# 128 rows a transfer in three unrolled loops of gathers and scatters (a graph and mixture-of-experts kernel)

## The reference, cut to what matters

```
# layer 0, graph step: two table rows for each node, by its degrees
x + z_in[in_deg] + z_out[out_deg] + cent_term + vor_term + sum3d

# layer 1, experts: 8 experts, the best 2 of each node, 256 -> 512 -> 256
xn = layernorm(x) * gamma + beta
top-2 of xn @ Wr gives two experts and two shares for each node
y_e = gelu(xn @ W1[e] + b1[e]) @ W2[e] + b2[e]
x + share0 * y_(expert 0) + share1 * y_(expert 1)
```

## Time and profile before

| what | value |
|---|---|
| median of 3 runs | 7661.86 us (7650.2, 7661.86, 7663.13) |
| the profiled execution | 7653.44 us |
| its span, first to last instruction | 7651.7 us |
| mean granted clock of TensorE | 0.787 |
| POOL busy | 3770.9 us, 49% |
| PE busy | 3976.6 us, 52% |
| DVE busy | 3494.0 us, 46% |
| DMA packets | 406511, 665.78 MB, mean 87 GB/s |

### The profile page before, as it was taken

The page is one execution under the profiler, slowest core; times in us unless marked ns, Lnnn a source line. Parts: engine busy times, 40 slices in busy tenths (PEclk is TensorE's granted clock), DMA queues, the critical chain, the costliest instruction groups (busy, mean ns, idle before and its releaser), DMA issues. The chain is left out here.

```text
span 7651.7 us, 94951 instructions
## 1 busy us (share of the span) xinstructions
PE 3976.6 (52%) x18034; PEld 3067.9 (40%) x18035; DVE 3494.0 (46%) x6616; ACT 690.7 (9%) x1705; POOL 3770.9 (49%) x4068
## 2 busy tenths in 40 slices
PE   0005664566300488728936666666666566415980
PEld 0004553344100488617824444444444344214770
DVE  8889999522310266651134444444444242631112
ACT  0000001122100000002210000000000012212220
POOL 0027777777777673000037777777777500043016
PEclk9999999997555699859956676677677589657995
DMA  1013333333333577400023333333333500112113
GB/s 45 0 46 101 101 105 100 96 103 100 100 100 104 173 251 235 146 0 0 0 72 104 104 105 103 103 104 104 104 103 104 85 5 0 52 41 63 63 56 100
DMA packets 406511, 665.78 MB, mean 87 GB/s; under 512 B 230847, under 2 KB 260719, under 8 KB 393799
## 3 DMA queue, kind: packets, MB, share of 16 engines
q0 software_dynamic: 172768, 374.98, 17.3%
q1 hardware_dynamic: 233703, 290.37, 13.7%
HBM read 518.80 MB, written 145.91 MB: 87 GB/s over the span
## 5 line engine op out<-in xcount | busy, mean ns | idle before, releaser
L1394 POOL DMA_INDIRECT rows<-xn_rows,pw_in x1664 | 1610.5, 968 | 523.4 <-issue 490.5
L532 POOL DMA_INDIRECT rows_by_src<-ring,stage x1563 | 1515.7, 970 | 483.8 <-issue 462.9
L1527 PE MATMUL pg<-rows,hot 128*125 128x256 f32 x3328 | 1272.8, 535 | 786.7 <-DMA rows<-xn_rows,pw_in 389.4
L1527 PEld LDWEIGHTS pg<-rows,hot 128*125 128x125 f32 x3328 | 824.6, 266 | 1224.3 <-issue 1085.4
L993 PE MATMUL pw<-hot,win 128*128 128x125 f32 x3968 | 502.0, 294 | 685.0 <-DVE hot L948 577.7
L993 PEld LDWEIGHTS pw<-hot,win 128*128 128x128 f32 x3968 | 497.1, 210 | 690.4 <-issue 690.4
L1412 DVE TENSOR_TENSOR agg<-agg,pg 125x256 f32 x832 | 349.1, 420 | 715.8 <-PE pg L1527 702.1
L1453 DVE TENSOR_TENSOR hot<-ids,pw_in 128x250 f32<-128x250 int32 x832 | 345.5, 416 | 549.0 <-issue 507.9
L948 DVE SCALAR_TENSOR_TENSOR hot<-win,win_base,iota_f 128x1000 f32<-128x1000 f32 x248 | 322.2, 1300 | 567.1 <-issue 567.1
L705 PE MATMUL phist<-hi,lo 128*125 128x50 bf16 x3136 | 413.9, 281 | 219.4 <-DVE hi L555 219.4
L705 PEld LDWEIGHTS phist<-hi,lo 128*125 128x125 bf16 x3136 | 370.5, 222 | 264.1 <-issue 257.1
(11 more groups left out here) (404 smaller groups left out, 6179.9 us busy)
## 6 DMA issues: line engine op xcount, KB each, us to landing
win<-rows_by_src SPq DMA_DIRECT2D x248, 516.0 KB, 4.8
ring<-in_edge_attr SPq DMA_DIRECT2D x97, 1024.0 KB
rows<-xn_rows,pw_in POOLq DMA_INDIRECT x1664, 2.8
rows_by_src<-ring,stage POOLq DMA_INDIRECT x1563
XT<-moe_rows SPq DMA_DIRECT2D x56, 256.0 KB, 2.6
moe_results<-XT POOLq DMA_DIRECT2D x56, 256.0 KB, 2.4
pw_in<-pairs_by_dst SPq DMA_DIRECT2D x832, 2.0 KB
e_w<-in_L_ffn_W SPq DMA_DIRECT2D x16, 512.0 KB
```

Source lines behind the costliest of these rows:

```text
L532: pool.indirect_dma_start(rows_d, bass.IndirectOffsetOnAxis(ap=stage[:, h * HC + j:h * HC + j + 1].bitcast(U32), axis=0), ring4[:, h, j, : ...
L1394: pool.indirect_dma_start(rows[:, (2 * (s % RU) + r) * D:(2 * (s % RU) + r + 1) * D], None, xn2_d, bass.IndirectOffsetOnAxis(ap=pw_in[:, s ...
L1527: mm = pe.matmul(pg[0:P, s % 4, 0:D], hot[:, ((s % 4) * 2 + r) * P:((s % 4) * 2 + r + 1) * P], rows[:, (2 * (s % RU) + r) * D:(2 * (s % RU ...
```

## The change

In all three places the index tile has 128 partitions instead of 125, and so has the tile that rows are gathered into. Three spare rows ride along in each transfer: in the gathers they read row 0 of the table (the index tiles are cleared first), in the scatter each writes to a row of its own behind the used part of `moe_rows`, which grows by 12800 rows. The index is taken from `z_idx`, `pos_x` and `pos_y` where DVE wrote it, and the scatter reads its rows from `XT` where ACT keeps them; the staging copies, the `xr` copies by ACT and their semaphores are gone. The loops are Python loops with constant wait values. The z rows have four buffers instead of two, with three tiles gathered ahead.

Added: POOL clears `XT[96:128]` (32 partitions by 12800 numbers) at the head of the experts' block one, ahead of the clearing of `zero`, and ACT waits for it before it stores into `XT`; POOL fills `pos_x` with an `iota` and clears `pos_y`; a clearing of `z_idx` in the first section.

```
-    moe_x_d = nc.dram_tensor("moe_rows", (2 * N + MW, D), ...)
+    moe_x_d = nc.dram_tensor("moe_rows", (2 * N + MW + 128 * NT * 2, D), ...)
# first section
+            sp.wait_ge(pads_set, 8)
+            pool.memset(z_idx[:], 0).then_inc(pads_set, 1)
# z gathers
-            def gather_z(t, u):
-                ch.step(pool.tensor_copy(z_stage[:, 2 * u:2 * u + 2], z_idx[:, bass.ds(t * 2, 2)]))
+            def gather_z(t):
+                if t >= ZU:
+                    pool.wait_ge(z_added, t - ZU + 1)
+                u = t % ZU
                 for k, name in enumerate(("L0_gnn_z_in", "L0_gnn_z_out")):
                     pool.indirect_dma_start(z_rows[...], None, a[name],
-                        bass.IndirectOffsetOnAxis(ap=z_stage[:, 2 * u + k:2 * u + k + 1].bitcast(U32), axis=0)
+                        bass.IndirectOffsetOnAxis(ap=z_idx[:, 2 * t + k:2 * t + k + 1].bitcast(U32), axis=0)
                         ).then_inc(z_rows_in[u], 16)
+            def add_z(t):
+                u = t % ZU
+                pool.wait_ge(z_rows_in[u], 32 * (t // ZU + 1))
+                pool.tensor_tensor(Rt(t), Rt(t), z_rows[0:P, 2 * u * D:(2 * u + 1) * D], ALU.add).then_inc(z_in_added, 1)
+                pool.wait_ge(z_in_added, t + 1)
+                pool.tensor_tensor(Rt(t), Rt(t), z_rows[0:P, (2 * u + 1) * D:(2 * u + 2) * D], ALU.add).then_inc(z_added, 1)
+            for t in range(ZU - 1):
+                gather_z(t)
+            for t in range(NT):
+                if t + ZU - 1 < NT:
+                    gather_z(t + ZU - 1)
+                add_z(t)
# experts, block one, POOL
+                pool.memset(XT[96:128, :], 0.0).then_inc(spare_set, 1)
+                pool.wait_ge(spare_set, 1)
                 pool.memset(zero[:], 0.0).then_inc(zero_set, 1)
+                pool.iota(pos_x[:], pattern=[[128, NT * 2]], base=2 * N + MW, channel_multiplier=1).then_inc(spare_set, 1)
+                pool.memset(pos_y[:], 0).then_inc(spare_set, 1)
                 pool.wait_ge(placed, 1)
-                def scatter(t, u, i):
-                    at(pool, xr_ready, t + 1, passed["pool"])
-                    ch.step(pool.tensor_copy(stage[:, 2 * u:2 * u + 2], pos_x[:, bass.ds(t * 2, 2)]))
+                pool.wait_ge(xn_kept, NT)
+                for t in range(NT):
                     for k in range(2):
-                        pool.indirect_dma_start(moe_x_d, ...stage[:, 2 * u + k:2 * u + k + 1]..., xr[:, u * D:(u + 1) * D], None)
+                        pool.indirect_dma_start(moe_x_d, ...pos_x[:, 2 * t + k:2 * t + k + 1]..., XT[:, t * TS:t * TS + D], None)
# experts, block one, ACT
+                act.wait_ge(spare_set, 1)
-                def send(t, u, i):
-                    if later(t):
-                        at(act, row_sent[u], i * 32, passed["act"])
-                    act.copy(xr[:, u * D:(u + 1) * D], kept(t)).then_inc(xr_ready, 1)
-                tiles(act, send)
# experts, block three, POOL
-                    ch.step(pool.tensor_copy(stage[:, 2 * u:2 * u + 2], pos_y[:, bass.ds(t * 2, 2)]))
+                for t in range(NT):
+                    u = t % 4
+                    if t >= 4:
+                        pool.wait_ge(yg_used, t - 3)
                     for k in range(2):
                         pool.indirect_dma_start(yg[...], None, moe_y_d,
-                            ...stage[:, 2 * u + k:2 * u + k + 1]...)
+                            ...pos_y[:, 2 * t + k:2 * t + k + 1]...)
```

More of the change, by code:

```diff
@@ L875, in program @@
         win_in = [sem(f"win_in{s}") for s in range(U)]
-        z_rows_in = [sem("z_rows_in0"), sem("z_rows_in1")]
-        z_added = sem("z_added")
+        z_rows_in = [sem(f"z_rows_in{u}") for u in range(ZU)]
+        z_in_added, z_added = sem("z_in_added"), sem("z_added")
         accs_ready = sem("accs_ready")
@@ L1912, in _ @@
             def _(pool):
-                ch = chain("pool", pool)
+                pool.memset(XT[96:128, :], 0.0).then_inc(spare_set, 1)
+                pool.wait_ge(spare_set, 1)
                 pool.memset(zero[:], 0.0).then_inc(zero_set, 1)
+                pool.iota(pos_x[:], pattern=[[128, NT * 2]], base=2 * N + MW, channel_multiplier=1).then_inc(spare_set, 1)
+                pool.memset(pos_y[:], 0).then_inc(spare_set, 1)
                 pool.wait_ge(placed, 1)
-                def scatter(t, u, i):
-                    at(pool, xr_ready, t + 1, passed["pool"])
-                    ch.step(pool.tensor_copy(stage[:, 2 * u:2 * u + 2], pos_x[:, bass.ds(t * 2, 2)]))
+                pool.wait_ge(xn_kept, NT)
+                for t in range(NT):
                     for k in range(2):
-                        pool.indirect_dma_start(moe_x_d, bass.IndirectOffsetOnAxis(ap=stage[:, 2 * u + k:2 * u + k + 1].bitcast(U32), axis=0),
-                                                xr[:, u * D:(u + 1) * D], None).then_inc(row_sent[u], 16)
-                tiles(pool, scatter, ch, 2)
-                for u in range(2):
-                    pool.wait_ge(row_sent[u], 32 * (NT // 2))
+                        pool.indirect_dma_start(moe_x_d, bass.IndirectOffsetOnAxis(ap=pos_x[:, 2 * t + k:2 * t + k + 1].bitcast(U32), axis=0),
+                                                XT[:, t * TS:t * TS + D], None).then_inc(row_sent, 16)
+                pool.wait_ge(row_sent, 16 * 2 * NT)
             @block.vector
@@ L2000, in pick @@
                     ch.step(dve.tensor_reduce(got[:], p3, AX.X, ALU.add))
-                    ch.step(dve.tensor_copy(out[:].rearrange("p (t k) -> p t k", k=2)[:, :, k], got[:]))
+                    ch.step(dve.tensor_copy(out[0:P, :].rearrange("p (t k) -> p t k", k=2)[:, :, k], got[:]))
+                dve.wait_ge(spare_set, 3)
                 for k in range(2):
@@ L2185, in program @@
         with ExitStack() as c3:
-            yg = sbuf(c3, "e_yg", [P, 4 * 2 * D])
-            stage = sbuf(c3, "e_stage2", [P, 4 * 2], I32)
+            yg = sbuf(c3, "e_yg", [128, 4 * 2 * D])
             yg_in = [sem(f"e_yg_in{u}") for u in range(4)]
@@ L2210, in _ @@
             def _(pool):
-                ch = chain("pool", pool)
-                def gather(t, u, i):
-                    if not isinstance(t, int) or t >= 4:
-                        at(pool, yg_used, t - 3, passed["pool"])
-                    ch.step(pool.tensor_copy(stage[:, 2 * u:2 * u + 2], pos_y[:, bass.ds(t * 2, 2)]))
+                for t in range(NT):
+                    u = t % 4
+                    if t >= 4:
+                        pool.wait_ge(yg_used, t - 3)
                     for k in range(2):
                         pool.indirect_dma_start(yg[:, (2 * u + k) * D:(2 * u + k + 1) * D], None, moe_y_d,
-                                                bass.IndirectOffsetOnAxis(ap=stage[:, 2 * u + k:2 * u + k + 1].bitcast(U32), axis=0)
+                                                bass.IndirectOffsetOnAxis(ap=pos_y[:, 2 * t + k:2 * t + k + 1].bitcast(U32), axis=0)
                                                 ).then_inc(yg_in[u], 16)
-                fours(pool, gather, ch, 1)
             @block.vector
```

44 lines of the change are left out of this document (12 added, 32 removed).

## The result

The changed kernel takes 7561.42 us (median of 4 runs, 7553.38 to 7568.24) against 7662.49 for the kernel before in the same company: ratio 0.987, 95% interval 0.9853 to 0.9887. That is 101 us less, where 131 were forecast. The range ended at 7562 us; the ratio, carried over to the 7661.86 us of the runs shown, gives 7562.3, just above it. The profiled execution took 7562.53 us with a span of 7560.8, 90.9 us less than the span before.

The account below looks back on a forecast made before the run. POOL's issue of indirect DMAs was taken to bound scatters and last block; 66 + 64 + 2 - 1 = 131 us less gave 7522 against the profiled 7653.4, 7531 carried to the median; forecast 7529, range 7505 to 7562.

Parts of the forecast that it names:

- The reading of the bound: Scatters and last block: POOL's issue of indirect DMAs sets the pace, 3.8 us a tile in each.
- harmless wait: Last block: POOL's wait for the tile four back is met near 6.5 us, before the buffer is needed at 10 us.
- The new price: Scatters and last block: a 128-row transfer costs POOL 1.25 us with idle, bounds 1.24 and 1.49.
- Scatters: Experts' scatters, first staging copy to last issue: 190.6 us becomes 125.6; 66 us less with landing, bounds 42 and 67.
- Last block: Last block's gathers: 188.8 us becomes 124.1, landing about 1 less, 2 off for queueing; 64 us less, bounds 35 and 67.
- z: Hidden z gathers: dropping 25.3 us of POOL's copies makes the stage 2 us less, bounds 3 more to 4 less.
- Its cover: z gathers: POOL would be done near 2850 us, still ahead of DVE's tables, which run to 3190.
- the port: z gathers: POOL's work slows DVE's tables by 12.4 us over the stage; fewer copies give back 2 us.
- Added work: Head of the experts' block one, mainly clearing `XT[96:128]` beside DVE's statistics: costs 1 us, bounds 0 and 5.
- A: Last block: the DMA engines take POOL's place; at 3.0 us a tile 25 us are lost, 7554; chance 0.12.
- B: Scatters and last block: issues get no cheaper with 128 rows; 200 transfers at 0.24 us, 48 us, 7577; chance 0.05.
- C: Scatters: unpaced transfers hold each other up in POOL's issue; slower from 2.6 us each, 7684 at 2.8; chance 0.01.
- D: Unrolled code must be fetched and POOL stands at times: 5 to 10 us, 7537; within the forecast case's 0.80.

Follow-up runs that it names:

- r3: Kernel before with the scatters' part alone (128 rows, unrolled, cleared `XT[96:128]`, larger `moe_rows`): 7593.29 us, ratio 0.9919.
- r9: Kernel before with the z gathers' part alone (128 rows, unrolled, four buffers, memset of `z_idx`), timed again: 7668.14 us, ratio 1.0035.
- r14: Kernel before with the z gathers unrolled, four buffers, indices from `z_idx`, but 125 rows and no memset: 7678.65 us, ratio 1.0039.
- r12: The whole change, timed again beside the parts, against the kernel before: 7549.58 us, ratio 0.9868.
- r10: Kernel before with the scatters' and last block's parts, without the z part: 7525.54 us, ratio 0.9838.
- r15: Changed kernel plus 15 one-column POOL memsets after that of `z_idx` and 11 after the z gathers: 7548.65 us, ratio 0.9868 to the kernel before.
- r16: Kernel before with the scatters' and last block's parts, without the z part, once more: 7534.81 us, ratio 0.985.
- r5: Kernel before with the z gathers' part alone, including the memset of `z_idx`, on a slower chip: 9832.81 us, ratio 1.0013.
- r13: Kernel before with only `z_idx` at 128 partitions and cleared by one more POOL memset: 7650.29 us, ratio 0.9999.
- r7: Changed kernel with 125 rows in each of the three transfers, on a slower chip: 9704.69 us, ratio 0.9892 to the kernel before.
- r11: Kernel before with 480 one-column POOL memsets behind the z loop: 7650.48 us, ratio 1.0.
- r17: Kernel before with 243 one-column POOL memsets behind the z loop, on a slower chip: 9813.73 us, ratio 1.0002.
- r18: Kernel before with the z part's three more semaphores and larger `z_rows` allocated but unused, on a slower chip: 9801.54 us, ratio 0.9993.
- r2: The changed kernel, unchanged, timed again against the kernel before: 7548.08 us, ratio 0.9863.

## Why the prediction was wrong

**The reading of the bound** was right: POOL's row of instructions set both stages, and shortening it shortened them. `yg_used` stayed the harmless wait it was taken for: POOL waited 1.5 us for DVE in the whole last block.

**The new price.** Forecast 1.25 us a transfer; measured 127.5 / 99 = 1.288 in the scatters and 1.284 in the last block. The idle of 0.30 was right. The issue was read at its tight end (0.95 in a stretch of the gathers) and came at 0.98, as the means of the earlier trace rows had said. 0.036 x 200 is 7 us of the shortfall.

**Scatters**: 66 forecast, 57.6 in the trace (62.3 - 4.7) and 57.7 in r3. Beside the pace, the term had landing 0.9 us shorter, which came as 1.7, and no drain: that is a step that failed too, a wait put at nothing. POOL's drain of 100 transfers of 128 rows took 6.2 us more. It wasn't seen because the prediction followed the chain to the landing and stopped there; the barrier's own instructions were not read.

**Last block**: 64 forecast, 60.8 in the trace between its issues. POOL's drain ends the program there:

```profile
L2175 POOLq DRAIN  x1: 14070/14070/14070, 7546.5 to 7546.5; - x1
L2175 SPq DRAIN  x1: 7/7/7, 7559.7 to 7559.7; - x1
```

It starts while POOL still has issues to make and ends 8.22 us after the last of them does, in all nine traces with this block, the same 8.22 us as in block one, with the landing and SP's last store beside it. SP is done at 7559.7, 8.3 us behind the last issue instead of 8.8, but the program ends 9.4 us behind it instead of 9.0. So the 1 us that earlier landing was to give did not arrive. (The term's own lower bound is added up wrongly: 188.8 - 147.8 + 1 - 5 is 37, not 35; nothing rests on it.)

**z: "2 us less (3 more to 4 less)" is the step that failed.** Its cover was read rightly: POOL's last z addition ends at 2852 us instead of 2965, near the 2850 that were forecast; the hot rows take 606.1 and 609.4 us, and over the 14 profiled executions of 7535 to 7675 us 596 to 615 with the unrolled z transfers and 598 to 608 without. Groups by line of POOL in the changed kernel, 2583 to 2966 us, beside the earlier trace rows:

```profile
L910 POOL DMA_INDIRECT z_rows<-in_L_gnn_z_in,z_idx x50 | 65.9, 1318 | 13.5 <-POOL R L919 12.5 <-issue 1.1
L910 POOL DMA_INDIRECT z_rows<-in_L_gnn_z_out,z_idx x50 | 59.5, 1189 | 15.2 <-issue 15.2
```

DVE's tables in two stretches, with and without POOL's z transfers, beside the earlier trace rows:

```profile
2583.00:2850.00 267.00, 142.47 (x104) 0.85 0.79 263
2860.00:3190.00 330.00, 170.17 (x136) 0.91 0.67 218
```

The copies are gone, and the z transfers are done in 267 us instead of 382. A table takes 142.47 / 104 = 1.370 us beside them and 170.17 / 136 = 1.251 after: 0.119 x 104 = 12.4 us in all, just what it was. So the port, by which POOL's work slows DVE's, gave nothing, where 2 us were forecast. The loss is elsewhere: a kernel with the unrolled z transfers has longer issues in one or both of the two stages that POOL paces with 3227 issues in all. Five comparisons of timed runs give its price: 18 (r9) and 27 us (r14), both clear of noise, 24 (r12 over r10), whose intervals just part, 14 (r15 over r16), whose intervals overlap a little, and 0.13% on the slower chip (r5), whose interval touches no change. The bounds of "3 more" came from the port alone, the one way in which the stage itself could be hurt; that an edit in a hidden stage could reach stages before and behind it was not among the steps.

**Why the issues get longer is open.** Shown not to be it: the memset of `z_idx` (r13), the larger `moe_rows` (r3, r10), the number of POOL's unrolled transfers (r10 has 200 and none of it), the rows in them (r7, r14), 480 and 243 instructions more (r11, r17), the loops' place modulo 16 (r15), and the semaphores and buffers by themselves (r18). It appears before the first z transfer has run, and it repeats from chip to chip, so it is a property of the program as laid down and not of what runs beside. It also isn't one fixed price: the z part alone (r5, r9) has it in the edge rows, the kernels with all three parts in the gathers, r14 in both. Where a program's parts lie in memory could do that; this wasn't tried.

**Added work.** Clearing `XT[96:128]` took 10.76 us and was done by 6644.9, ACT's first store came at 6657.5. The head up to the first scatter got 0.7 us shorter. The staging copy that no longer stands ahead of that scatter had taken 0.9 (6768.96 to 6769.84), so all added work cost 0.2 us where 1 was taken off.

**The rivals.** A: no. The last block carries a DMA share of 0.51 at 152 GB/s, with gathers landing in 3.5 us and POOL held up for 1.5. By the Trainium skill's rule ("DMA: Bandwidth & Descriptors", section "Why a DMA increments its semaphore by 16 and not by 1") a store of 125 rows goes to five engines; no run here shows that they were crowded. B: no, by r7. C: no, unpaced scatters have a median issue of 972 ns, and the last is as short as the others, at a DMA share of 0.29. D: not in the changed kernel, where no gap inside the scatters or the last block is above 0.31 us. The Trainium skill ("Runtime: NRT & Kernel Launch", section "Instruction fetch mechanics") says that straight code is fetched ahead; the trace agrees, with 0.30 us ahead of each issue. But r7, on its slower chip, has two gaps in its unrolled scatters, 39 issues apart, that end with no wait that the profile shows:

```profile
8962.84 1.18 POOL L1919 DMA_INDIRECT moe_rows<-XT,e_pos_x  x1 [3.67 <-issue]
9024.00 1.18 POOL L1919 DMA_INDIRECT moe_rows<-XT,e_pos_x  x1 [3.55 <-issue]
```

They are the single gaps of some us that D foretold; no run shows what POOL stood for in them.

With the pace at 1.288 and the drain in the sum, the forecast without z would have been 129 - 7 - 6 = 116 us, and r10 and r16 measured 124 and 117. The rest, 14 to 24 us, is the z part. The range would have held the pace and the drain; with z it did not hold.

## What to carry over

Price a change where the kernel is bound by issues in the mean of the long stages, not in their quietest stretch, and read the barrier's drain behind the last landing before giving the chain a length. A part of a change that is "hidden anyway" should be timed by itself: here it was the second smallest term of the sum and cost an eighth to a fifth of the gain, and leaving it out gives the fastest kernel of all (0.9838 and 0.985 against 0.9868). And a change of several things at once should be split: most of what was gained for each transfer came from dropping the staging copy and the loop's waits, not from the 128 rows.

## What the runs showed of the hardware

- An indirect transfer of 128 rows of 1 KB costs POOL 0.94 to 0.98 us to issue, one of 125 rows 1.18 to 1.21, with the same code around it (r7 against r2). The first makes 48 DMA packets, the second 128.
- POOL's drain at the end of a block, after all transfers have landed, takes 8.22, 4.62 and 4.14 us for 100, 56 and 50 transfers of 128 rows or partitions, and 1.85 and 2.02 us for 100 scatters of 125 rows. It does not go on growing like that: 8.81 us behind 1563 scatters of 516-byte rows. In the last block with 128 rows it ends 8.22 us after POOL's last issue, with the landing beside it.
- The length of an issue isn't a constant of the instruction: the gathers' median is 946 to 949 ns in some programs and 953 to 957 in others that differ elsewhere, the edge rows' 958 to 962 or 967, and one kernel moves by 3 to 4 ns from execution to execution.
